# Attention weights of a fused layer: staged through SBUF and VectorE, or cast by the DMA that loads them in the first chunk

## The reference

```python
def _rmsnorm(v, scale):
    n = jnp.sqrt(jnp.sum(v * v, axis=-1, keepdims=True)) * d ** (-0.5)
    return scale * v / (n + EPS)
xl, xr = jnp.split(x, 2, axis=-1)          # x is already layer-normed
xn = jnp.concatenate([_rmsnorm(xl, ls_scale), _rmsnorm(xr, rs_scale)], axis=-1) * split_scale
K = jax.nn.sigmoid(xn @ Wk)                # Wk 1024 x 2048
u, g_in, g_out = jnp.split(xn @ Wugg, 3, axis=-1)   # Wugg 1024 x 6144
u = u * jax.nn.sigmoid(g_in) * (1.0 - K)
_, h = jax.lax.associative_scan(combine, (a, u), axis=1)
y = (h * jax.nn.sigmoid(g_out)) @ Wout     # Wout 2048 x 1024
...
h = jax.nn.gelu(jnp.einsum('bsd,edf->bsef', x, W1) + b1)   # W1 4 x 1024 x 4096
expert_out = jnp.einsum('bsef,efd->bsed', h, W2) + b2      # W2 4 x 4096 x 1024
```

## Time and profile before

| | us |
|---|---|
| Median of the two runs shown | 6707.25 (6311.74 and 7102.76) |
| The profiled execution | 6314.33 |
| Its span on the slowest core, core 3 | 6312.7 |
| Spans of the eight cores | 6255.4 to 6312.7 |

### The profile page before, as it was taken

One profiled execution on the slowest core, in us unless ns is written; L12 is line 12 of the kernel. 1 busy time (PEld: TensorE's weight loads), 2 busy tenths in 40 slices (PEclk: granted clock), 3 DMA queues, 4 the chain that ended last, 5 costly groups with the idle time before them and its releaser, 6 DMA issues.

```text
span 6312.7 us, 64265 instructions; the slowest of 8 cores (6255.4 to 6312.7 us)
## 1 busy us (share of the span) xinstructions
PE 5046.9 (80%) x23137; PEld 2233.4 (35%) x23137; DVE 1313.5 (21%) x3372; ACT 1476.2 (23%) x2404; POOL 286.7 (5%) x455
## 2 busy tenths in 40 slices
PE   0066678787998788987898789987899878987998
PEld 0023233333343333433443334433344333433443
DVE  2133100043102410043111420033200431024000
ACT  1012122122231223122222222212322222212212
POOL 0000000000000000000000000000000000000000
PEclk9998888888999899997999889998999989998999
DMA  4657999942334243341444333341434323441343
GB/s 129 165 162 146 183 205 206 213 138 94 134 134 155 79 141 133 134 173 52 144 139 147 107 120 134 134 173 61 140 127 141 146 87 127 139 170 66 134 147 120
DMA packets 312544, 864.12 MB, mean 137 GB/s; under 512 B 84260, under 2 KB 117156, under 8 KB 258984
## 3 DMA queue, kind: packets, MB, share of 16 engines
q0 software_dynamic: 123424, 438.33, 24.9%
q1 hardware_dynamic: 97608, 333.58, 15.8%
q10 hardware_dynamic: 91200, 88.09, 4.4%
HBM read 826.39 MB, written 104.86 MB: 148 GB/s over the span
## 4 chain that ended last, share of the span: by engine, by line
PE 69%; DMA 12%; DVE 9%; ACT 5%; issue 4%; ACTq 1%; DVEq 1%; POOL 0%; SPq 0%; POOLq 0%
PE pb L838 26%; PE pb L787 26%; PE pb L525 13%; DMA slab<-W 5%; PE pb L633 3%; DMA sWA<-h_sb 3%; DMA sW<-slab 2%; DMA h_sb<-sWA 1%; ACT tmpev L856 1%; ACT tmpev L852 1%; DMA slab<-sW 1%; ACTq L289 1%; DVE h_sb L282 1%; DVE stv L651 1%; DVEq L87 1%
## 5 line engine op out<-in xcount | busy, mean ns | idle before, releaser
L787 PE MATMUL pb<-xnf2h,slab 128*128 128x512 bf16 x8192 | 1867.2, 392 | 163.7 <-DMA slab<-W 73.9
L838 PE MATMUL pb<-slab,h_sb 128*128 128x512 bf16 x8192 | 1839.2, 388 | 196.4 <-ACT xnf L441 71.3
L787 PEld LDWEIGHTS pb<-xnf2h,slab 128*128 128x128 bf16 x8192 | 817.0, 100 | 1210.2 <-issue 330.9
L838 PEld LDWEIGHTS pb<-slab,h_sb 128*128 128x128 bf16 x8192 | 813.3, 100 | 1218.7 <-issue 323.9
L799 ACT ACTIVATE h_sb<-pb,b1s 128x512 bf16<-128x512 f32 x1024 | 704.0, 688 | 1119.4 <-PE pb L787 1109.0
L525 PE MATMUL pb<-xnf,slab 128*128 128x512 bf16 x3200 | 702.8, 380 | 301.6 <-DMA slab<-sWA 296.1
L861 DVE TENSOR_TENSOR acc<-acc,tmpev 128x1024 f32<-128x1024 f32 x128 | 156.8, 1225 | 2353.8 <-ACT tmpev L856 2353.6
L525 PEld LDWEIGHTS pb<-xnf,slab 128*128 128x128 bf16 x3200 | 307.4, 98 | 696.0 <-issue 340.6
L852 ACT ACTIVATE tmpev<-pb,wsb 128x512 f32<-128x512 f32 x128 | 88.0, 687 | 1803.2 <-PE pb L838 1782.0
L525 PE MATMUL pb<-xnf,h_sb 128*128 128x512 bf16 x896 | 227.5, 420 | 113.0 <-DMA h_sb<-sWA 97.6
L309 POOL DMA_DIRECT2D slab<-sW x224 | 144.5, 645 | 3769.5 <-PE pb L787 1814.2
(11 more groups left out here) (130 smaller groups left out, 1926.7 us busy)
## 6 DMA issues: line engine op xcount, KB each, us to landing
slab<-sW SPq DMA_DIRECT2D x224, 1024.0 KB, 5.2
slab<-sW POOLq DMA_DIRECT2D x224, 1024.0 KB, 5.6
slab<-W POOLq DMA_DIRECT2D x64, 1024.0 KB, 23.2
sW<-slab ACTq DMA_DIRECT2D x64, 1024.0 KB, 13.0
slab<-sWA SPq DMA_DIRECT2D x50, 1024.0 KB, 6.9
slab<-sWA POOLq DMA_DIRECT2D x50, 1024.0 KB, 6.4
x_sb<-x_in POOLq DMA_DIRECT2D x32, 512.0 KB, 6.1
sWA<-h_sb ACTq DMA_DIRECT2D x128, 128.0 KB, 6.0
```

What stands on the lines that cost most here:

```text
L787: e.matmul(pb[bk][:, 0:512], lhsT=slab[:, sl, (kc * 4 + jp) * 128:(kc * 4 + jp) * 128 + 128], rhs=xnf2h[:, kc, :], start=(kc == 0), stop=( ...
L838: e.matmul(pb[m * 2 + h][:, 0:512], lhsT=h1_sb[:, j, m * 128:(m + 1) * 128], rhs=slab[:, sl, jj * 1024 + h * 512:jj * 1024 + h * 512 + 512 ...
```

## The change

The 32 cast jobs, their semaphores and their order are taken out. In chunk 0 each attention piece j is built in its slot by four cast loads on GpSimd's DMA queue, one for Wk and one for each part of Wugg, each of 128 partitions by 8 row blocks by 128 columns (512 bytes of float32 in a run, 256 bytes of bf16). One store of 1 MB to `sWA[j]` follows on ScalarE's queue, after which chunks 1 to 7 load the piece as before. The weights are now stored without the scale. The scale is applied instead where the transposed rows leave PSUM: in `emit_ln1_tr` one ScalarE copy of 128 by 512 becomes four ScalarE activations of 128 by 128, each with its own scale column. That is so in all 8 chunks.

```diff
-        cast_jobs = []
...
-        def cast_step():
...
         def ensure_region(region):
-            while any(j[0] == region for j in cast_jobs[cast_state["i"]:]):
-                cast_step()
-            return region_done[region]
+            return [t for t in region_done[region] if t is not None]
...
+        wk_p = wk_in.rearrange("(k p) c -> p k c", p=128)
+        wugg_p = wugg_in.rearrange("(k p) (w jc) -> p k w jc", p=128, w=3)
+
+        def load_piece_cast_wa(j):
+            s = slot_rr[0]
+            slot_rr[0] = (s + 1) % 4
+            slab4 = slab[:, s, :].rearrange("p (k w c) -> p k w c", w=4, c=128)
+            p.op("gpsimd",
+                 lambda e, slab4=slab4, j=j: e.dma_start(
+                     out=slab4[:, :, 0, :], in_=wk_p[:, :, j * 128:(j + 1) * 128]),
+                 waits=[slot_free[s], store_free[s]], inc=f"dZ{s}")
+            tokL = None
+            for w in range(3):
+                tokL = p.op("gpsimd",
+                            lambda e, slab4=slab4, j=j, w=w: e.dma_start(
+                                out=slab4[:, :, w + 1, :],
+                                in_=wugg_p[:, :, w, j * 128:(j + 1) * 128]),
+                            inc=f"dZ{s}")
+            tokS = p.op("scalar",
+                        lambda e, s=s, j=j: e.dma_start(
+                            out=sWA[j].rearrange("p k w c -> p (k w c)"),
+                            in_=slab[:, s, :]),
+                        waits=[tokL], inc=f"dT{s}")
+            store_free[s] = tokS
+            region_done.setdefault("WA", [None] * 4)[s] = tokS
+            return s, tokL
...
-                ev = p.op("scalar",
-                          lambda e, half=half, mt=mt, bk=bk:
-                          e.copy(xnf[:, half * 4:half * 4 + 4, mt * 128:(mt + 1) * 128],
-                                 pbb[bk][:, 0:512].rearrange("p (q c) -> p q c", q=4)),
-                          waits=[tk], inc="Sc")
+                for q in range(4):
+                    kc = half * 4 + q
+                    ev = p.op("scalar",
+                              lambda e, kc=kc, q=q, mt=mt, bk=bk:
+                              e.activation(xnf[:, kc, mt * 128:(mt + 1) * 128],
+                                           pbb[bk][:, q * 128:(q + 1) * 128],
+                                           AF.Copy, scale=sc_sb[:, kc:kc + 1]),
+                              waits=[tk, tSc] if q == 0 else [], inc="Sc")
...
+                elif ch == 0:
+                    sl, tokL = load_piece_cast_wa(j)
...
-                if ch == 0:
-                    for _ in range(2):
-                        cast_step()
```

More of the change, by code:

```diff
@@ L130, in build_program @@
     p.sem("dC", "sync", 16)
[L131 to L137, removed]
     for _s in range(4):
@@ L203, in build_program @@
         sems = {n: E(nc.semaphore(n)) for n in
[4 rows of a table removed]
-                 + ["dW" + _r for _r in CAST_REGIONS])}
-        h1f32 = h1_sb[:].rearrange("p a b -> p (a b)").bitcast(F32)
+                ["dC", "dP0", "dP1", "dP2", "dP3",
+                 "dT0", "dT1", "dT2", "dT3", "dZ0", "dZ1", "dZ2", "dZ3",
+                 "dQ0", "dQ1", "dQ2", "dQ3", "dU0", "dU1", "dU2", "dU3",
+                 "dX0", "dX1", "dY", "T", "V", "Sc", "G"]}
         h1b16 = h1_sb[:].rearrange("p a b -> p (a b)")
@@ L265, in build_program @@
-        cast_state = {"i": 0, "cin_free": [None, None], "st2": [None, None]}
-        region_done = {}
-        def cast_step():
[L269 to L294, removed]
@@ L553, in build_program @@
                 p.op("vector", lambda e, jb=jb, pbase=pbase:
-                     e.tensor_mul(u1t[:, jb, :], pb[pbase + 1][:, 0:512], tmpgin[:, jb, :]),
-                     waits=(list(cast_state["st2"]) if (ch == 1 and j == 0) else []))
+                     e.tensor_mul(u1t[:, jb, :], pb[pbase + 1][:, 0:512], tmpgin[:, jb, :]))
                 p.op("vector", lambda e, jb=jb:
@@ L793, in build_program @@
                         gw = [tmm7, tB1s]
-                        if ch == 0 and e_ == 0 and j == 0:
-                            gw += list(region_done["WA"])
-                            gw += list(cast_state["cin_free"])
                         gel_tok[j] = p.op("scalar",
```

## The result

| | before | after |
|---|---|---|
| Median of all runs, us | 6725.5 (10 runs, 6304 to 7112) | 6515.5 (11 runs, 6150 to 6953) |
| Profiled execution | 6314.3 | 6154.7 |
| Ratio, after to before | | 0.9757, 95% interval 0.9735 to 0.9779 |

The change makes the kernel 2.4% faster, about 155 us (159.7 between the two profiled executions).

A forecast was written before the change was run, and what follows sets the result against it. The cast jobs were taken as a serial prelude that keeps TensorE waiting 296 us. The sum was 6314 - 232 for the earlier mark + 70 for the scaled copies = 6152 us, in a range from 6085 to 6300.

The forecast's parts named there:

- the mark: Start of the first product with Wout in chunk 0: from 496 to 264 us, a gain of 232 us.
- Step 1: Chunk 0's norm: copies 2.3 us longer in each of four serial tiles, so the first matmul starts at 87.5 us.
- Step 2: First four attention pieces of chunk 0: loads run from about 20 us and have landed by 56, under the norm.
- Step 3: Period of an attention piece in chunk 0: 12.0 us, load 8.9 plus store 3.1.
- my lower extrapolation: Cost of a piece's added small packets, from the old 256-byte stores: 4 ns more per packet, 0.8 us.
- Step 4: Pieces 4 to 15 of chunk 0: DMA sets the pace from 97 us; piece 15 lands at 247, sigmoids and gate end at 261.
- Step 5: Wout's fourth load in chunk 0: lands at 269 where the product wants it at 267; 3 us added, mark at 264.
- a packet of over 46 ns: Sign in the profile after that the forecast is wrong; 25 to 45 ns was expected for queue 0's added 256-byte packets.
- The scaled copies: On TensorE's path: 9.2 us in each of chunks 1 to 6, 5 in chunk 0, 10 for the clock; 70 us together.
- Dear packets: Rival, chunk 0's piece loads: period of 15 to 24 us, 46 to 82 ns a packet; 6248 us at 20; chance 25%.
- Packets equal at any length: Rival, chunk 0's piece loads: 108 ns a packet, period 31 us, mark at 525, total 6413 us; chance 9%.
- Full-width copies: Rival, norm's copies: scaled copies cost like full-width operations, 2.4 us more a half tile, total 6229 us; chance 10%.

The follow-up runs named there:

- The two halves run alone: Changed kernel with the new loads but the old plain copies: 6088 us; kernel before with only the scale moved to four scaled activations: 6397 us against 6316.
- the multiply: Changed kernel with the four ScalarE activations of a half tile replaced by one VectorE multiply with broadcast scale columns: 6139 us against 6150.
- the new order: Changed kernel with the next chunk's norm work reordered, so that transposes come before the next tile's norm in experts 1 and 2: 6084 us.
- the three together: Changed kernel with eight slot-free loads and stores on SyncE's queue, reordered norm work, and one VectorE multiply for four activations: 5967 us against 6310 before.

## Why the prediction was right or wrong

**The number given for the time was wrong.** I forecast 6152 us, in a range from 6085 to 6300, and the median of the runs is 6515.5. The step that failed is in the sum: "I compare with the execution that has a profile." The number belongs to executions like that one, and there it holds (6154.7). But the table of before already had a second run of 7103 us and a median of 6707, and I put at nothing, without a reason, that the runs of the changed kernel would spread as widely. They do: eleven runs lie between 6150 and 6953, ten of before between 6304 and 7112. Taken from the median shown instead, the same 162 us give 6545, and a range up to the upper runs, some 6950, would have been honest. The difference survives such a base; the level doesn't. Why runs of one kernel lie so far apart was not asked by any experiment here and stays open.

**The difference was right, and so were most of its terms; two errors in the mark cancelled by luck.**

- *Step 1, the norm.* First matmul at 87.5 forecast, 84.6 measured. The copies lengthened as worked out: one scaled activation takes 367 ns (forecast 370), as the profile's row says:

```profile
L420 ACT ACTIVATE xnf<-pb,sc_sb x256: 367/367/368, 36.9 to 5381.4; 128x128 bf16<-128x128 bf16 x128
```

  What I missed is that the norm starts about 3 us earlier, because the small constant loads land earlier (at 22.2 us, 25.1 before). That this comes from the plain 1 MB loads of the old jobs, which are no longer beside them, is likely and not shown.

- *Step 2.* Pieces 0 to 3 had landed at about 57 us, as forecast: in the DMA view of 20 to 60 us the rate falls to nothing there. Right.

- *Step 3, the period,* 12.0 forecast, 11.5 from matmul to matmul and 11.0 by bytes. The load by itself was nearly right: 8.9 forecast, 9.2 measured. What was mis-sized is the addition: load 8.9 plus store 3.1. Where the two run side by side, most of the time of the small packets doesn't come on top: 0.2 to 0.5 us a piece against the 2.0 that I had put in. That is less even than my lower extrapolation, 0.8 us, from the old 256-byte stores. On the other side the base was larger: 10.8 us even with the packets of W1, where I had taken 10.0 from the experts.

- *Step 4* has the second error, of the other sign. By its terms piece 5 lands at about 97 + 2 x 12 = 121; its matmuls start at 131.2. I had looked at the store of slot 0 alone. On core 0 the store of slot 1 is issued at 97.3, behind ScalarE's sigmoids, and lands at 107.8; only then is piece 5's load issued, at 108.3. After that ten periods take 114.5 us instead of 120, Wout's loads in the last of them included, and piece 15 starts at 245.7 where 247 was forecast. That the two errors met is luck.

- *Step 5.* The mark was forecast at 264; on core 3, the core of before's profile, it is at 263.7. But Wout's loads come late: the first product stops twice for them (4.46 and 4.03 us on core 0), where I had allowed 3 in all. On core 3 the product's sum is taken up by VectorE at 283.1, where it was 505.7. So of the 232 us at the mark 223 are left behind it.

- *The packet's time in the page.* I had said that a packet of over 46 ns would prove me wrong. In the window 97 to 260 us a packet of queue 0 took 0.974 x 16 x 163 / 51156 = 50 ns, and yet the period is under 12. The shares of the queues sum to 126% there: packets overlap. Where that is so, packet time times count isn't throughput; bytes over time is.

- *The Trainium skill's rules* (DMA: Bandwidth & Descriptors, Specifications and Why small descriptors are slow). That runs under 512 bytes move at less than full rate agrees in direction: loads that write runs of 256 bytes have 114 to 119 GB/s by themselves, those that write 1 KB 144 to 151. The size is not that of a doubling, 9.2 us for 7.1. The estimate that I had worked out from 3 bus cycles a packet, a load of 5.7 us, is too short: the measured 9.2 decides.

- *The scaled copies,* 9.2 us a chunk and the clock at expert 3. From the end of the up products to line 813 (838) TensorE takes 14.8, 11.2 and 4.7 us in experts 1 to 3, where it took 10.1, 8.9 and 2.3 (medians over cores and chunks 1 to 6): 4.7, 2.3 and 2.4 more, for 4.6, 2.3 and 2.3. In expert 1 only 2.3 of these stand right before line 813, the rest between the transposes, where TensorE waits for the copies of the tile before. Expert 3's last wait was forecast to become 4.2 us and is 4.21; the clock fell as supposed, and expert 3's matmuls take 57.88 instead of 55.43 us, 2.4 where I had 1.5 to 1.8. In sum 69.6 for 65. The two halves run alone confirm it.

- *The rivals.* Dear packets: no. Packets equal at any length: no; with 8192 in a load the whole loses only some 20 us. Full-width copies: no, 367 ns. (By the prediction's own terms equal packets would turn to a loss at a period of 25, not 24; nothing hangs on it.)

## What to carry to other kernels

Before costing a stage, look at what the last operation in it waits for and whether the work in between is needed by it: here a reordering of two lists, found only because the copies' price was looked for, was worth as much as the copies cost. When work is moved off one engine, look at that engine's place in the new queue; a cheaper operation (the multiply) gained nothing until the order was right. A load priced by itself and a store priced by itself don't add up to the pace of both: here 7.1 and 9.2 us for the load alone became 10.8 and 11.0 beside the stores. And when the runs shown are far apart, say which of them the number is for, and make the range for what will be measured.

## What the hardware showed that I had not expected

GpSimd issued 15 weight loads of 1024 packets before the first of them had landed (23.2 us), and then stood idle for 12.2 us ahead of the sixteenth, though that one waits for nothing in the program. It went out at 31.33, when four had landed, the fourth at 30.92. The other cores did the same, with the sixteenth between 30 and 33 us. The kernel before never had so many under way.

```profile
17.22 1.90 POOL L292 DMA_DIRECT2D slab<-Wugg  x2
31.33 0.88 POOL L292 DMA_DIRECT2D slab<-Wugg  x1 [12.22 <-issue]
```

The same 15 went ahead in the run with 256-byte runs, also of 1024 packets each; there the sixteenth followed at 34.3 us, when eight had landed. What frees the place isn't told by this. Here the hold cost nothing, since GpSimd does nothing else; in a kernel that computes on it, it would.

In experts 1 to 3 of chunks 1 to 6, over all cores of the kernel before, the kernel after, the new order and the three together, TensorE's granted clock in the 4 us behind the wait ahead of line 838's (813's) matmuls was 1.00 in 189 of 192 places where this wait was 1.2 to 1.9 us, and 0.50 to 0.67 in all 384 where it was 3.1 to 11.2 us, with short transposes before it. The 256 matmuls took 55.4 us in the first case and 56.7 to 58.4 in the second, so that a wait 2 us shorter gave about 2 us more. The wait's length alone doesn't decide it: in expert 0 it is 2.0 us and the clock stays low behind it (0.50 to 0.67), and there, on every core of the kernel after, it was at 0.50 already in the 4 us ahead.
